# Edge ranks from (window, segment) partitions and a segment pick, in a one-core graph network kernel

## The chip, the cores and the metric

The kernel runs on one core of a Trainium2 chip. The metric is device time in microseconds, the median of three runs. Times of single instructions come from one profiled execution of the same program.

## The reference

One layer of a graph network with 3125 nodes of 64 features, 53125 edges (25000 in both directions and a self loop at each node) and hidden width 128. Every edge has a source `src`, a destination `dst` and a weight.

```
h   = silu(concat(x[src], x[dst], edge_weight) @ eW1 + eb1)   # 53125 x 128
m   = silu(h @ eW2 + eb2)                                     # 53125 x 128
agg = segment_sum(m, src, 3125)
y   = silu(concat(x, agg) @ nW1 + nb1) @ nW2 + nb2
out = layernorm(x + y)
```

The random `src` is not sorted, so the sum over edges needs the edges brought into an order by source on the chip.

## The kernel before

**Layout.** The edges lie on 125 partitions (EP) and 425 columns (ECOL). The columns are cut into 9 chunks, `LOAD = [50, 30, 38, 44, 48, 54, 54, 54, 53]`. A node's number is 25 x `lo` + window, 25 windows (WIN) in all. A counting sort on the chip brings the edges of a window together in tiles of 128 slots (SLOT). There are 440 tiles in 110 groups of four (GT). For every tile GpSimd gathers 128 rows of the table `q_table` (x times the destination half of eW1) by an indirect DMA; TensorE adds the source half by one-hot products with `p_table`, runs the two edge layers and sums each tile's edges into its window (`segment`), which VectorE adds into `agg`.

**Parts of the sort.** `part(name, k, i)` issues a step of the sort of chunk k, on VectorE and on TensorE. On VectorE, before:

- MATCH (line 1048) compares every edge's window `win_b` with the 25 windows: `in_win`, 25 x columns elements on each of the 125 partitions.
- SCAN (1061) is a running sum over `in_win`, two instructions: `count`.
- TOTAL (1065 to 1070) takes the end of each window's run: `total`, `rank`.
- TensorE's OFFSET multiplies `total` by `before` (earlier partitions) and by `ones` (all of them).
- OFFSET (1074 to 1093) makes `base`: the first place of each window in each partition, with the tile in multiples of ENC = 8192.
- SUM adds `base` to `count` (1105), multiplies by `in_win` (1109, 1110) and reduces over the 25 windows (1111), in two halves of the columns: `slot`.
- SLOTS (1116 to 1126) splits this into tile, row and column; DEST and WINDOW place the chunk's tiles in the order of windows.
- SORT makes one-hots of column and row for batches of six columns (`col_hot` 1209, `row_hot` 1210, `load_hot` 1215) in a ring of three; TensorE's `sort(k, i)` multiplies them. CLOSE ends the chunk's product, READ takes the gather indices `q_index` (1247) and the weights out.

**Order.** The tables VECTOR and TENSOR, written by `plan()`, say at which of the 110 steps a part stands on its engine. At step m TensorE issues `second_layer(m-2)`, `first_layer(m)`, `turn(m+2)`, `segment(m-4)` and then its parts; VectorE issues `one_hots(m+3)`, `add_segments(m-5)` and its parts. `first_layer(m)` reads the four gathered tiles of group m. GpSimd's buffer holds four groups, so the gathers of group g wait for the first layer of step g-4; a new chunk waits for `index_ready`, group 2 for chunk 1's offsets and group 3 for chunk 1's WINDOW as well.

**Start.** ScalarE loads its table, clears `agg` and copies results. TensorE transposes x (line 795), takes OFFSET of chunk 0 after the first of the P/Q products (`pq`, `less`), runs these for 13 pairs of windows, and from slot 10 on puts chunk 0's sort batches between them. ScalarE copies each P/Q result out (534, 536), and among these copies writes the columns of `load` (489) that VectorE's first sort batch needs. GpSimd derives the node numbers of chunks 1 to 8 (713 to 722) once VectorE's first one-hots are done (`hots_ready`).

Of the kernel before, what the change touches and what calls it, by code (L numbers as in the profile page):

```python
# [31 lines left out]
EVEN = [n + n % 2 for n in LOAD]  # L32
# [17 lines left out]
CMAX, NMAX, BATCH = max(COLS), max(EVEN), 6  # L50
V = 4
# [3 lines left out]
WSPLIT = [(0, HALF), (HALF, WIN)]  # L55
# [9 lines left out]
assert sum(LOAD) == ECOL and TILES % GT == 0 and all(n % 2 == 0 for n in LOAD[:-1]) and V * CMAX <= 512  # L65
# [10 lines left out]
def batches(k):  # L76
# [27 lines left out]
def plan():  # L104

    at(TENSOR, 0, (CARRY, 1, 0))
    sorts(1, [0, 0, 0, 1, 1], [0, 0, 0, 1, 1])
    at(TENSOR, 1, (CLOSE, 1, 0))
    at(VECTOR, 2, (READ, 1, 0), (MATCH, 2, 0), (SCAN, 2, 0))
    at(VECTOR, 3, (SCAN, 2, 1), (TOTAL, 2, 0), (ENCODE, 2, 0))  # L110
    at(TENSOR, 3, (OFFSET, 2, 0))
    at(VECTOR, 4, (OFFSET, 2, 0), (SUM, 2, 0))
    at(TENSOR, 4, (DEST, 2, 0))
    at(VECTOR, 5, (SUM, 2, 1), (DEST, 2, 0), (SLOTS, 2, 0))
# [3 lines left out]
    sorts(2, [5, 6, 6, 7, 7, 8, 8], [6, 6, 7, 7, 8, 8, 8])  # L118
    at(TENSOR, 8, (CLOSE, 2, 0))
    at(VECTOR, 9, (READ, 2, 0), (MATCH, 3, 0), (SCAN, 3, 0), (SCAN, 3, 1), (TOTAL, 3, 0))  # L120
    at(TENSOR, 9, (OFFSET, 3, 0))
    at(VECTOR, 10, (OFFSET, 3, 0), (SUM, 3, 0))
    at(TENSOR, 10, (DEST, 3, 0))
    at(VECTOR, 11, (DEST, 3, 0), (SUM, 3, 1))
    at(TENSOR, 11, (WINDOW, 3, 0))
    at(VECTOR, 12, (WINDOW, 3, 0), (SLOTS, 3, 0))
    at(TENSOR, 12, (CARRY, 3, 0))
    sorts(3, [12, 12, 13, 13, 14, 15, 15, 16], [13, 13, 14, 14, 15, 16, 16, 16])
    at(TENSOR, 16, (CLOSE, 3, 0))

    at(VECTOR, 17, (READ, 3, 0), (MATCH, 4, 0))
    at(VECTOR, 18, (SCAN, 4, 0), (SCAN, 4, 1), (TOTAL, 4, 0))
    at(TENSOR, 18, (OFFSET, 4, 0))
    at(VECTOR, 19, (OFFSET, 4, 0), (SUM, 4, 0))
    at(TENSOR, 19, (DEST, 4, 0))
    at(VECTOR, 20, (DEST, 4, 0), (SUM, 4, 1))
    at(TENSOR, 20, (WINDOW, 4, 0))
    at(VECTOR, 21, (SLOTS, 4, 0), (WINDOW, 4, 0))
    at(TENSOR, 21, (CARRY, 4, 0))
    sorts(4, [21, 22, 22, 23, 24, 24, 25, 26], [22, 23, 23, 24, 25, 25, 26, 27])  # L140
    at(TENSOR, 27, (CLOSE, 4, 0))
# [78 lines left out]
def build(nc, x, src, dst, edge_weight, eW1, eb1, eW2, eb2, nW1, nb1, nW2, nb2, out):  # L220
    with ExitStack() as ctx:
# [6 lines left out]
        def sem(name):  # L228
# [10 lines left out]
        iota_w = sb("iota_w", [EP, WIN, 2], BF16)  # L239
# [6 lines left out]
        before = sb("before", [128, 128])  # L246
        ones = sb("ones", [128, 128])
# [28 lines left out]
        win_b = sb("win_b", [EP, ECOL + 1], BF16)  # L276
# [68 lines left out]
        window_ps = [t[0:1, 128:256] for t in flat_ps]  # L345

# [19 lines left out]
        iota_w_c = const_ps[0:EP, 128:128 + WIN].bitcast(BF16).rearrange("p (b e) -> p b e", e=2)  # L366
        base_c = const_ps[0:EP, 160:160 + WIN]
# [3 lines left out]
        def load_c(c):  # L371
# [7 lines left out]
                 "totals_ready offsets_ready dest_ready dests_ready upto_ready window_ready window_read rest_ready restT_ready "  # L379
# [6 lines left out]
         totals_ready, offsets_ready, dest_ready, dests_ready, upto_ready, window_ready, window_read, rest_ready, restT_ready,  # L386
# [8 lines left out]
        FILLS = 6  # L395
# [70 lines left out]
        def _(act):  # L466
# [10 lines left out]

            act.wait_ge(fills_ready, 1)
# [60 lines left out]
            for i in range(PQ_SLOTS):  # L539
# [93 lines left out]
            load_coded(1)  # L633
            for m in range(GROUPS):
# [55 lines left out]
        def _(pool):  # L690
# [4 lines left out]
            fills = [(ones[:], 1.0), (run_prev[:], 0.0), (carried[:], 0.0), (win_b[:, ECOL:ECOL + 1], -1.0),  # L695
# [53 lines left out]
        def _(pe):  # L749
# [71 lines left out]
            for i in range(PQ_SLOTS):  # L821
# [164 lines left out]
        def _(dve):  # L986
# [11 lines left out]
            def then(ins):  # L998
                done(mark(ins))
# [437 lines left out]
```

## Time and profile before

| what | us |
|---|---|
| median of 3 runs (lowest, highest) | 629.42 (627.53, 630.96) |
| the profiled execution | 630.7 |
| its span | 628.9 |
| TensorE busy | 533.6 (85%) |
| VectorE busy | 462.9 (74%) |
| GpSimd busy | 430.5 (68%) |
| ScalarE busy | 355.5 (57%) |

The span runs from the first to the last instruction of the profiled execution; the run's own time is 1.8 us longer. Busy shares are means over the whole span. GpSimd's busy time holds neither the issue of its gathers nor its waits. What a stage is bound by is read from windows of time and from what ended each wait.

### The profile page before, as it was taken

What the parts mean: (1) busy time and instruction counts of PE and PEld (TensorE: products, weight loads), DVE (VectorE), ACT (ScalarE), POOL (GpSimd) and SP (SyncE); (2) the same over time, 40 slices, a digit from 0 to 9 for tenths busy, and PEclk for the clock granted to TensorE, in tenths of its full rate; (3) what the DMA queues carried; (4) which work ended last, traced back from release to release, by engine and by line L of the source; (5) the groups of instructions that cost most, each with busy time, mean ns of one, the idle gap of its engine ahead of it and who ended that gap; (6) DMA issues with size and microseconds to landing.
All of it is one profiled execution on the core that took longest, in us unless ns stands there. A gap on an engine that the chain in (4) does not pass through costs nothing.

```text
span 628.9 us, 15166 instructions
## 1 busy us (share of the span) xinstructions
PE 533.6 (85%) x4653; PEld 449.0 (71%) x4653; DVE 462.9 (74%) x1364; ACT 355.5 (57%) x812; POOL 430.5 (68%) x465
## 2 busy tenths in 40 slices
PE   3953979779889979999998899889997888879695
PEld 2432768758768868887787788778776777769584
DVE  5998999988999898999788868797642533223356
ACT  4852555535645656665555555565556666556464
POOL 2327677566777777777777777777777777777750
PEclk9985889879989999999999999999999999999998
DMA  5121111111211112212121112111221212111111
GB/s 121 58 63 53 48 51 53 39 46 48 56 52 52 53 51 56 55 49 55 53 56 52 55 51 58 53 54 51 56 53 55 56 52 55 52 55 56 52 39 51
DMA packets 17215, 34.17 MB, mean 54 GB/s; under 512 B 8133, under 2 KB 9352, under 8 KB 17142
## 3 DMA queue, kind: packets, MB, share of 16 engines
q0 software_dynamic: 14080, 28.86, 16.8%
q1 hardware_dynamic: 2594, 3.40, 2.1%
q10 hardware_dynamic: 468, 0.96, 0.6%
q8 instruction: 43, 0.70, 0.5%
q14 instruction: 30, 0.25, 0.1%
HBM read 30.73 MB, written 2.40 MB: 53 GB/s over the span
## 4 chain that ended last, share of the span: by engine, by line
POOL 33%; DVE 27%; PE 18%; issue 16%; DMA 4%; DVEq 2%; ACTq 0%; SPq 0%
POOL q_rows L738 33%; PE layer_ps L751 7%; PE sort_ps L751 5%; PE seg_ps L751 4%; DVE load_hot L1215 3%; DVE agg L1286 3%; DMA q_rows<-q_table,q_index 3%; DVE hot L1271 2%; DVE count L1061 2%; DVE place L1105 2%; DVE col_hot L1209 1%; DVE row_hot L1210 1%; DMA x_sb<-in_x_dram 1%; DVEq L1278 1%; DVE slot L1111 1%
## 5 line engine op out<-in xcount | busy, mean ns | idle before, releaser
L738 POOL DMA_INDIRECT q_rows<-q_table,q_index x440 | 420.8, 956 | 155.0 <-issue 128.5
L585 ACT ACTIVATE e<-layer_ps 128x512 f32<-128x512 f32 x110 | 65.7, 597 | 212.5 <-PE seg_ps L751 207.4
L1286 DVE TENSOR_TENSOR agg<-agg,seg_ps 128x125 f32 x416 | 93.1, 280 | 95.2 <-PE seg_ps L751 92.0
L751 PE MATMUL layer_ps<-hotT,p_table 128*128 128x128 bf16 x1320 | 160.0, 225 | 0.1
L751 PE MATMUL layer_ps<-ident_f,q_rows 128*128 128x128 f32 x440 | 127.1, 289 | 34.7 <-DMA q_rows<-q_table,q_index 34.2
L751 PE MATMUL seg_ps<-hot,e 128*128 128x125 f32 x880 | 124.6, 285 | 19.4 <-DVE agg L1286 19.3
L751 PEld LDWEIGHTS layer_ps<-hotT,p_table 128*128 x1320 | 122.8, 99 | 23.6 <-issue 2.3
L751 PEld LDWEIGHTS seg_ps<-hot,e 128*128 128x128 f32 x880 | 109.0, 195 | 22.5 <-issue 20.3
L751 PE MATMUL layer_ps<-w_sb,h 128*128 128x128 f32 x880 | 120.0, 280 | 0.0
L751 PEld LDWEIGHTS layer_ps<-w_sb,h 128*128 128x128 f32 x880 | 111.6, 194 | 4.7 <-issue 0.2
L751 PEld LDWEIGHTS layer_ps<-ident_f,q_rows 128*128 128x128 f32 x440 | 63.3, 144 | 45.6 <-DMA q_rows<-q_table,q_index 43.8
L1215 DVE TENSOR_TENSOR load_hot<-col_hot,const_ps 125x2448 bf16<-125x2448 bf16 (+9 forms) x73 | 93.7, 1283 | 0.0
L751 PE MATMUL sort_ps<-load_hot,row_hot 125*128 125x408 bf16 (+5 forms) x425 | 82.7, 336 | 9.5 <-DVE load_hot L1215 9.5
L579 ACT ACTIVATE h<-layer_ps,eb_sb 128x512 f32<-128x512 f32 x110 | 76.0, 691 | 16.3 <-PE layer_ps L751 16.2
L565 ACT ACTIVATE hot<-hot 128x500 f32<-128x500 bf16 x110 | 69.0, 628 | 0.0
L624 ACT ACTIVATE layer_ps<-b_sb 128x512 f32<-128x512 f32 x110 | 67.0, 609 | 0.1
L573 ACT ACTIVATE hotT<-turn_ps 128x512 bf16<-128x512 bf16 x110 | 64.9, 590 | 3.7 <-PE turn_ps L843 3.7
L751 PEld LDWEIGHTS sort_ps<-load_hot,row_hot 125*128 125x128 bf16 x425 | 41.6, 101 | 34.7 <-issue 9.3
L1271 DVE TENSOR_TENSOR hot<-const_ps,lo 128x512 bf16<-128x512 bf16 x110 | 45.9, 418 | 24.7 <-ACT hot L565 24.0
L843 PE MATMUL turn_ps<-ident_b,hot 128*128 128x128 bf16 x440 | 43.6, 223 | 0.9 <-ACT hot L560 0.8
L1210 DVE TENSOR_TENSOR row_hot<-const_ps,row 125x768 bf16<-125x768 bf16 (+2 forms) x73 | 39.0, 535 | 0.0
L1209 DVE TENSOR_TENSOR col_hot<-const_ps,col 125x612 bf16<-125x612 bf16 (+9 forms) x73 | 31.9, 437 | 2.6 <-PE sort_ps L751 2.0
(193 smaller groups left out, 432.1 us busy)
## 6 DMA issues: line engine op xcount, KB each, us to landing
q_rows<-q_table,q_index POOLq DMA_INDIRECT x440
q_table<-q_in_sb SPq DMA_DIRECT2D x1, 784.0 KB
x_sb<-in_x_dram ACTq DMA_DIRECT2D x1, 700.0 KB
q_table<-q_in_sb SPq DMA_DIRECT2D x1, 616.0 KB
out_dram<-x_sb SPq DMA_DIRECT2D x2, 224.0 KB
out_dram<-x_sb SPq DMA_DIRECT2D x1, 252.0 KB
w_in<-in_edge_weight_dram SPq DMA_DIRECT2D x1, 185.9 KB
dst_i<-in_dst_dram SPq DMA_DIRECT2D x1, 185.9 KB
```

Source lines behind the costliest of these rows:

```text
L565: A.activation(hot32[:, g % 4], hot[:, g % HOT_RING, :, 0:LO], ACT.Copy).then_inc(hot32_ready, 1)
L573: A.activation(hotT[:, g % TURNED, :], hotT_ps, ACT.Copy).then_inc(hotT_ready, 1)
L579: A.activation(h1[:, m % 2, :], pre_of(m)[:], ACT.Silu, bias=eb1_sb[:, 0:1]).then_inc(h1_ready, 1)
L585: A.activation(e2[:, m % 2, :], e_of(m)[:], ACT.Silu).then_inc(e2_ready, 1)
L624: A.activation(e_of(m)[:].rearrange("p (j f) -> p j f", j=GT), b2_sb[:].unsqueeze(1).to_broadcast([128, GT, HID]), ACT.Copy).then_inc(bias ...
L738: P.indirect_dma_start(q_rows[:, g % RING, j, :], None, q_table, bass.IndirectOffsetOnAxis(ap=q_index[:, GT * g + j:GT * g + j + 1], axis= ...
L751: return nc.tensor.matmul(o, lhsT, rhs, start=start, stop=stop, **kw)
L843: last = nc.tensor.transpose(hotT_ps[:, j * 128:(j + 1) * 128], hot[:, g % HOT_RING, j, :], ident_b[:])
L1210: D.tensor_tensor(pairs(row_hot[:, q, 0:m, :]), iota(SLOT), each(row2[:, a:a + m, :], SLOT), ALU.is_equal).then_inc(hots_ready, 1)
L1215: D.tensor_tensor(load_hot[:, q, 0:m, :, 0:c].rearrange("p m v (a b) -> p m v a b", b=2), pairs(col_hot[:, q, 0:m, 0:c]).unsqueeze(2).to_b ...
L1271: D.tensor_tensor(pairs(hot[:, g % HOT_RING]), iota1_c.rearrange("p (a b) -> p a b", b=2).unsqueeze(1).to_broadcast([128, GT, 64, 2]), lo2 ...
L1286: D.tensor_tensor(o, o, seg_ps[:, j * LO:(j + 1) * LO], ALU.add).then_inc(agg_added, 1)
```

## The change

The 125 partitions stand for 25 windows times SEG = 5 segments of the columns when ranks are counted, instead of for 125 rows of edges.

- A chunk's windows `win_b` are transposed by TensorE (`turn_windows`), chunk 0 as its first instruction, chunks 1 to 8 ahead of chunk 0's third last sort batch. `spread_windows` multiplies them by `column_sel`, a table of ones that ScalarE writes at the start, LOAD/5 products of 125 x 125: after that every partition (segment, window) sees all edges of its segment. ScalarE copies the result from PSUM into `spread` (chunk 0 is read from PSUM by VectorE).
- MATCH compares with one number for each partition (`win_col`); `in_win` has 25 x columns elements as before. SCAN is one instruction with f32 output, TOTAL one operation. OFFSET has two operations more (`own`, `base_col`); its product uses `upto_sel` in place of `before`.
- SUM becomes two `scalar_tensor_tensor` operations, (count + base_col) x in_win. TensorE's `pick(k)` reduces over windows and brings the places back to edge order: LOAD/5 f32 products of 125 x 125 by 125 x 5 (`seg_sel`). SLOTS reads them from PSUM; it waits for `slots_ready` and, from chunk 1 on, for `dests_ready`.
- `LOAD` is `[50, 30, 45, 50, 50, 50, 50, 50, 50]`, and `plan()` follows: chunk 3's READ is at step 18 (17 before), chunk 4's at 29 (28 before).
- GpSimd's derivation of later node numbers waits no more for `hots_ready`, only for the landed data.

```diff
-LOAD = [50, 30, 38, 44, 48, 54, 54, 54, 53]
+SEG = 5
+LOAD = [50, 30, 45, 50, 50, 50, 50, 50, 50]
...
             pool.wait_ge(src_rest_in, 32)
-            pool.wait_ge(hots_ready, 1)
...
+            act.wait_ge(ident_ready, 2)
+            A.activation(column_sel[:], ident_b[0:NMAX, 0:NMAX].unsqueeze(2).to_broadcast([NMAX, NMAX, WIN]), ACT.Copy) \
+                .then_inc(column_sel_ready, 1)
             act.wait_ge(fills_ready, 1)
             clear(agg[0])
...
+            def turn_windows(chunks):
+                for k in chunks:
+                    last = nc.tensor.transpose(win_t_ps(k), win_b[:, COL0[k]:COL0[k] + NMAX], ident_b[0:EP, 0:EP])
+                last.then_inc(win_t_ready, 1)
+            def spread_windows(k, i):
+                pe.wait_ge(win_turned, 1 + (k > 0))
+                if k >= 2:
+                    pe.wait_ge(w_parted, k - 1)
+                    pe.wait_ge(spread_read, fill_of(k, i) - 1)
+                sel = column_sel[:].rearrange("q c b -> q (c b)")
+                for t0, n, bank in spread_columns(k, i):
+                    for t in range(n):
+                        last = mm(bank[:, t, :], sel[0:LOAD[k], (t0 + t) * EP:(t0 + t + 1) * EP], win_t[0:LOAD[k], k, :], True, True)
+                last.then_inc(spread_made, 1)
+            def pick(k):
+                n = segments(k)
+                for t in range(n):
+                    if t in (0, n // 2):
+                        pe.wait_ge(place_ready, 2 * k + 1 + (t > 0))
+                    last = mm(slot_ps[k % 2][:, t * SEG:(t + 1) * SEG], count[:, t * EP:(t + 1) * EP], seg_sel[:], True, True)
+                last.then_inc(slots_ready, 1)
...
                 elif name == SUM:
-                    halves = [(0, m // 2), (m // 2, m)]
...
+                    half = segments(k) // 2 * EP
+                    for a, b in ((0, half), (half, wide)):
+                        D.scalar_tensor_tensor(count[:, a:b], count[:, a:b], base_col[:, 0:1], in_win[:, a:b],
+                                               ALU.add, ALU.mult).then_inc(place_ready, 1)
```

At the start of TensorE's program, before: x is transposed, then `sort_ps<-total` is OFFSET of chunk 0, and `layer_ps<-w_sb,xT` are the P/Q products.

```order
L795 MATMUL layer_ps<-ident_f,x_sb 128x125 x12
L795 MATMUL seg_ps<-ident_f,x_sb 64x125
L751 MATMUL layer_ps<-w_sb,xT 125x512
L751 MATMUL sort_ps<-total,before 125x25
L751 MATMUL sort_ps<-total,ones 125x25
L751 MATMUL layer_ps<-w_sb,xT 125x512
L751 MATMUL layer_ps<-p_table,minus_b 125x256
```

In the changed kernel the same place reads so; `win_t,column_sel` is the spread and `seg_sel,count` the pick.

```order
L829 MATMUL turn_ps<-ident_b,win_b 50x125
L812 MATMUL sort_ps<-win_t,column_sel 125x125 x8
L812 MATMUL turn_ps<-win_t,column_sel 125x125 x2
L896 MATMUL layer_ps<-ident_f,x_sb 128x125 x8
L812 MATMUL sort_ps<-total,upto_sel 125x25
L812 MATMUL sort_ps<-total,ones 125x25
L896 MATMUL layer_ps<-ident_f,x_sb 128x125 x4
L896 MATMUL seg_ps<-ident_f,x_sb 64x125
L812 MATMUL layer_ps<-w_sb,xT 125x512
L812 MATMUL sort_ps<-seg_sel,count 125x5 x10
L812 MATMUL layer_ps<-w_sb,xT 125x512
```

OFFSET has moved ahead of the last five transposes of x, and the pick stands between the first and the second P/Q product.

At step 0 TensorE had, ahead of its first layer (`layer_ps<-ident_f,q_rows`), the turn of chunk 0's rest and OFFSET of chunk 1:

```order
L846 MATMUL turn_ps<-ident_b,rest 100x128
L751 MATMUL sort_ps<-total,before 125x25
L751 MATMUL sort_ps<-total,ones 125x25
L855 TENSOR_LOAD p_at
L751 MATMUL layer_ps<-ident_f,q_rows 128x128
```

In the changed kernel there stand at the same place the pick, DEST (`tiles_upto`, `dest_row`) and WINDOW (`ge`) of chunk 1 and the first spread of chunk 2 as well:

```order
L951 MATMUL turn_ps<-ident_b,rest 100x128
L812 MATMUL sort_ps<-total,upto_sel 125x25
L812 MATMUL sort_ps<-total,ones 125x25
L812 MATMUL sort_ps<-seg_sel,count 125x5 x6
L812 MATMUL sort_ps<-ones,tiles_upto 25x1
L812 MATMUL sort_ps<-ones,dest_row 100x1
L812 MATMUL sort_ps<-ge,ones 1x55
L812 MATMUL sort_ps<-win_t,column_sel 125x125 x4
L960 TENSOR_LOAD p_at
L812 MATMUL layer_ps<-ident_f,q_rows 128x128
```

DEST and WINDOW of chunk 1 have moved from behind step 0's work to ahead of its first layer.

On VectorE the sum of chunk 0 was, between the offset arithmetic and the first operation of SLOTS (`tile`):

```order
L1081 SCALAR_TENSOR_TENSOR base<-tiles_upto,base 125x25
L1105 TENSOR_TENSOR place<-count,base 125x625 x2
L1109 TENSOR_TENSOR place<-place,in_win 125x325
L1110 TENSOR_TENSOR place<-place,in_win 125x300
L1111 TENSOR_REDUCE slot<-place 125x25
L1109 TENSOR_TENSOR place<-place,in_win 125x325
L1110 TENSOR_TENSOR place<-place,in_win 125x300
L1111 TENSOR_REDUCE slot<-place 125x25
L1116 TENSOR_SCALAR tile<-slot 125x50
```

In the changed kernel there stands instead:

```order
L1197 SCALAR_TENSOR_TENSOR base<-tiles_upto,base 125x25
L1198 TENSOR_TENSOR own<-base,win_sel 125x25
L1199 TENSOR_REDUCE base_col<-own 125x1
L1223 SCALAR_TENSOR_TENSOR count<-count,base_col,in_win 125x625 x2
L1232 TENSOR_SCALAR tile<-sort_ps 125x50
```

Eight operations have become four, and `tile` reads TensorE's result.

## Rows read from the trace of the kernel before

**Rows 1.** GpSimd's timeline: start us, duration us, instruction, idle before and its releaser.

```profile
41.48 1.17 POOL L738 DMA_INDIRECT q_rows<-q_table,q_index  x1 [9.80 <-DVE q_index L1247]
...
119.17 0.95 POOL L738 DMA_INDIRECT q_rows<-q_table,q_index  x1 [3.55 <-PE seg_ps L751]
...
199.66 0.94 POOL L738 DMA_INDIRECT q_rows<-q_table,q_index  x1 [0.30 <-issue]
...
606.53 0.94 POOL L738 DMA_INDIRECT q_rows<-q_table,q_index  x1 [0.30 <-issue]
```

**Rows 2.** Waits of GpSimd, whole span: us in total, times, longest.

```profile
POOL q_rows L738 <- PE seg_ps L751: 14.7, 16, 3.5
```

**Rows 3.** Busy time by stretch: us, each engine's busy us, PEclk, DMA share, GB/s.

```profile
41.50:150.00 108.50, 81.23 (x689) 67.72 (x690) 100.04 (x312) 51.15 (x120) 74.85 (x78) 0.83 0.18 48
...
290.00:470.00 180.00, 166.44 (x1476) 139.82 (x1475) 141.65 (x395) 101.52 (x227) 136.13 (x144) 1.00 0.20 54
...
16.58:28.08 11.50, 11.50 (x40) 4.96 (x39) 11.09 (x26) 11.15 (x41) 1.89 (x3) 1.00 0.24 79
```

The engines stand in the order PE, PEld, DVE, ACT, POOL.

**Rows 4.** TensorE's timeline, columns as in rows 1.

```profile
9.95 2.76 PE L795 MATMUL layer_ps<-ident_f,x_sb 125*128 125x125 f32 x12 [9.95 <-DMA x_sb<-in_x_dram]
...
14.42 0.46 PE L751 MATMUL sort_ps<-total,before 125*125 125x25 f32 x2
15.13 1.51 PE L751 MATMUL layer_ps<-w_sb,xT 128*125 128x512 f32 x2
16.58 1.02 PE L751 MATMUL layer_ps<-w_sb,xT 128*125 128x512 f32 x2
...
28.08 0.94 PE L751 MATMUL sort_ps<-load_hot,row_hot 125*128 125x296 bf16 x6
...
32.67 0.94 PE L751 MATMUL sort_ps<-load_hot,row_hot 125*128 125x296 bf16 x6
...
113.39 0.40 PE L751 MATMUL sort_ps<-total,before 125*125 125x25 f32 x2 [3.22 <-DVE total L1069]
...
619.52 1.04 PE L751 MATMUL turn_ps<-n_sb,load_hot 128*125 128x64 f32 x8
```

**Rows 5.** ScalarE's timeline in the first 22 us, columns as in rows 1.

```profile
6.54 2.81 ACT L476 ACTIVATE agg<-ones 128x3125 f32<-128x3125 f32 x1
...
21.14 0.66 ACT L489 ACTIVATE load<-enc_i 125x100 bf16<-125x100 bf16 x3
```

**Rows 6.** VectorE's groups by line and form, 109 to 131 us: busy us, mean ns.

```profile
L1111 DVE TENSOR_REDUCE slot<-place 125x22 f32<-125x550 f32 x2 | 2.7, 1330 | 0.1
L1105 DVE TENSOR_TENSOR place<-count,const_ps 125x550 f32<-125x550 bf16 x2 | 1.4, 725 | 0.0
L1109 DVE TENSOR_TENSOR place<-place,in_win 125x286 f32<-125x286 f32 x2 | 0.9, 444 | 0.0
```

**Rows 7.** VectorE's timeline up to the first index, columns as in rows 1.

```profile
6.38 2.81 DVE L1061 TENSOR_TENSOR_SCAN count<-sort_ps,in_win 125x650 bf16<-125x650 f32 x2
...
15.34 0.18 DVE L1074 TENSOR_TENSOR summed<-carried,sort_ps 125x25 f32<-125x25 f32 x1 [3.48 <-PE sort_ps L751]
...
22.52 0.19 DVE L1116 TENSOR_SCALAR tile<-slot 125x50 f32<-125x50 f32 x1
...
24.62 0.37 DVE L1199 COPY const_ps<-load 125x200 f32<-125x200 f32 x1
...
37.28 0.38 DVE L1209 TENSOR_TENSOR col_hot<-const_ps,col 125x444 bf16<-125x444 bf16 x1
...
40.40 0.21 DVE L1247 TENSOR_SCALAR q_index<-sort_ps 128x49 int32<-128x49 int32 x1 [0.58 <-PE sort_ps L751]
```

**Rows 8.** Page, costliest groups: count, busy us, mean ns of one, idle before.

```profile
L1215 DVE TENSOR_TENSOR load_hot<-col_hot,const_ps 125x2448 bf16<-125x2448 bf16 (+9 forms) x73 | 93.7, 1283 | 0.0
...
L1210 DVE TENSOR_TENSOR row_hot<-const_ps,row 125x768 bf16<-125x768 bf16 (+2 forms) x73 | 39.0, 535 | 0.0
L1209 DVE TENSOR_TENSOR col_hot<-const_ps,col 125x612 bf16<-125x612 bf16 (+9 forms) x73 | 31.9, 437 | 2.6 <-PE sort_ps L751 2.0
```

More of the change, by code:

```diff
@@ L64 @@
 TAG = 1 << 29
-assert sum(LOAD) == ECOL and TILES % GT == 0 and all(n % 2 == 0 for n in LOAD[:-1]) and V * CMAX <= 512
+assert sum(LOAD) == ECOL and TILES % GT == 0 and all(n % SEG == 0 for n in LOAD) and SEG * WIN == EP and V * CMAX <= 512
 assert all(EP * COL0[k] // SLOT + FULL[k] <= TABLE for k in range(CHUNKS)) and EP * max(LOAD) + SLOT <= 8000
@@ L77, in batches @@
     return [(a, min(BATCH, LOAD[k] - a)) for a in range(0, LOAD[k], BATCH)]
-MATCH, SCAN, TOTAL, OFFSET, SUM, SLOTS, DEST, WINDOW, SORT, READ, CARRY, CLOSE, ENCODE, NODE_X, RESIDUAL, CARRIED = (
-    "match", "scan", "total", "offset", "sum", "slots", "dest", "window", "sort", "read", "carry", "close", "encode",
-    "node_x", "residual", "carried")
+SPREAD, MATCH, SCAN, TOTAL, OFFSET, SUM, PICK, SLOTS, DEST, WINDOW, SORT, READ, CARRY, CLOSE, ENCODE, NODE_X, RESIDUAL, CARRIED = (
+    "spread", "match", "scan", "total", "offset", "sum", "pick", "slots", "dest", "window", "sort", "read", "carry", "close",
+    "encode", "node_x", "residual", "carried")
 VECTOR, TENSOR = {}, {}
@@ L944, in _ @@
                     part(OFFSET, 1, 0)
+                    pick(1)
+                    part(DEST, 1, 0)
+                    part(WINDOW, 1, 0)
+                    spread_windows(2, 0)
                 first = first_layer(m)
@@ L1081, in part @@
                         then(D.scalar_tensor_tensor(base[:], tiles_upto[:], float(ENC), base[:], ALU.mult, ALU.add))
+                        then(D.tensor_tensor(own[:], base[:], win_sel[:], ALU.mult))
+                        then(D.tensor_reduce(base_col[:], own[:], AX.X, ALU.add))
                         return
@@ L1353, in _ @@
             encode(*CODED[0])
-            for name, i in ((OFFSET, 0), (SUM, 0), (SUM, 1), (SLOTS, 0)):
+            for name, i in ((OFFSET, 0), (SUM, 0), (SLOTS, 0)):
                 part(name, 0, i)
@@ L1365, in _ @@
             dve.wait_ge(rest_coded, 2)
-            for name, i in ((ENCODE, 0), (MATCH, 0), (SCAN, 0), (SCAN, 1), (TOTAL, 0), (OFFSET, 0), (SUM, 0), (DEST, 0), (SUM, 1),
-                            (SLOTS, 0), (WINDOW, 0)):
+            for name, i in ((MATCH, 0), (SCAN, 0), (TOTAL, 0), (ENCODE, 0), (OFFSET, 0), (SUM, 0), (SLOTS, 0), (DEST, 0),
+                            (WINDOW, 0)):
                 part(name, 1, i)
```

258 lines of the change are left out of this document (160 added, 98 removed).

## The prediction

> **What bounds the kernel now.** Read first the busy time by stretch, then GpSimd's waits and its row of gathers, then each engine's timeline up to the first gather.
>
> GpSimd issues 440 gathers, the first at 41.48 us, the last at 606.53 [rows 1]. A gather takes 0.94 us and the next follows after 0.30 of issue: 1.25 us each. So the span of 628.9 is 41.48 of prologue, 439 x 1.25 = 548.75 of gathers at full pace, 16.3 of excess over that pace, 0.94 for the last gather and 21.4 of tail. A change gains only by bringing the first gather forward, by taking from the 16.3, or in the tail, which this change leaves alone.
>
> Where the excess arises is read by index: gather 56 (group 14) starts at 119.17, that is 7.7 us behind 41.48 + 56 x 1.25; gather 116 (group 29) at 199.66, 13.2 behind [rows 1]. The last 3.1 come in 400 us, from somewhat longer gathers. TensorE ended 16 waits of GpSimd, 14.7 us with 4.8 of ordinary issue in them [rows 2]; with one more on a transpose, some 11.3 us are true waiting. The cause stands behind TensorE: VectorE is busy 100.04 of the 108.5 us after the first gather [rows 3], and the 3.55 us before gather 56 follow a TensorE queue that stood 3.22 us on VectorE's totals of chunk 3 [rows 1, 4]. After 290 us VectorE has slack (141.65 of 180) and TensorE, though 166.44 busy, ends no gather wait of weight.
>
> **The prologue: what is added.** VectorE can no longer match straight after its node numbers. TensorE turns and spreads them first, and its spread needs `column_sel` from ScalarE. ScalarE's first activation started at 6.54 and wrote 3125 columns in 2.81 [rows 5], 0.9 ns a column; the 1250 of `column_sel` end at about 7.85. Ten spread products at 0.14 us (six of 296 columns take 0.94 [rows 4]; bounds 1.1 to 2.1 in all) end at 9.25. The match reads 1250 f32 elements from PSUM: 0.73 us for 550 [rows 6] makes 1.5. The scan keeps its 1250 elements, 2.81 [rows 7], and ends at 13.75; its output is f32 now, which I price at nothing because the scan's own pace of 2.2 ns an element is far above any write seen here. Total at 13.95. Before, totals were ready by 9.9 and TensorE came for them only at 14.42 [rows 4], so this delay alone costs nothing there.
>
> The order on TensorE does cost. After totals: OFFSET 0.9, five x transposes 1.1 (twelve took 2.76), the first P/Q product 1.7: 17.7. VectorE's offset arithmetic took 1.28 from 15.34 to the sum; with two new short operations it ends at 16.6, and two `scalar_tensor_tensor` of 625 elements at 0.8 end at 18.2. Then come ten `pick` products ahead of the second P/Q product. The trace has no product with five moving columns. An f32 product is two passes; eight passes of 64 columns took 1.04, 0.13 each; two of 25 columns 0.40 to 0.46, no less [rows 4]. Early passes run slower (1.51 against 1.02 for the same pair [rows 4]). So 20 passes cost 2.6 to 3.9 us; I take 3.2, the middle, since the pace changes just there. End: 20.9.
>
> The Trainium skill, TensorE: Matmul & The Clock Gate, section LDWEIGHTS (loading the stationary operand), says that a weight load takes time by the stationary operand's columns, P/1.2 ns, whatever moves. That is 104 ns for 125 columns, 2.1 us for 20 passes as an estimate; the sum below would be 626.7 by it. The trace agrees that few columns don't make a pass cheap, but its passes are longer.
>
> The second P/Q product thus starts at 20.9 instead of 15.13; the product now runs at the full pace, 0.5 back: 5.3 late. TensorE was busy for all of the 11.50 us up to chunk 0's first sort [rows 3], so nothing absorbs the shift: that sort goes from 28.08 to 33.4, the third from 32.67 to 38.0 (done 38.8). VectorE makes the one-hots in a ring of three, so its sixth batch waits for the third sort. Before, VectorE ran free: first copy at 24.62, then 1.75 a batch, the eighth at 37.28 [rows 7]. The sixth thus began at 33.78, and now at 38.8: 5.0 late. ScalarE's load columns (21.14 [rows 5]) move by 5.3 as well, to 27.1 when written, later than VectorE's slots, which start 1.4 earlier than 22.52 [rows 7]; the ring is later still and decides. The first index, 40.40 [rows 7], moves by 5.1 with the turns and the second spread hidden in TensorE's gaps between VectorE-paced batches. **Prologue +5.1**, bounds +2.5 (pick at 2.6, spread at 1.1, VectorE at once behind) to +7.3 (pick at 3.9, spread at 2.1, and 0.7 for turns and spread that are not hidden). GpSimd's node work beside the scan is in these bounds: it has only to be done by the seventh sort batch, and it touches the chain only if it slows the 2.81 us scan.
>
> **The loop: what is removed.** For chunk 3, the sum was two adds of 0.725, four products of some 0.44 and two reductions of 1.33 [rows 6]: 5.9 us. Now two operations of 0.8. Totals take one operation instead of five (0.46 less), the base two more (0.4): 4.3 less on VectorE. But chunks grow: a batch of six columns costs 1.28 + 0.54 + 0.44 = 2.26 [rows 8], 0.38 a column. Chunk 2 gets seven more: 3.6 saved, 3.0 given back. Chunk 3 gets six more: 4.3 saved at steps 9 to 12, 2.6 back at steps 13 to 16. Chunk 1 saves 3.1 and gives back 1.5 on the wait for `pick`. Chunk 4, two columns more, saves 4.0. So VectorE is ahead by some 2.3 us at step 9, 6 at step 13, 4 at step 17 and 8 at step 28.
>
> New on the other side: DEST, WINDOW and `pick` of chunk 1 now stand ahead of step 0's first layer on TensorE, and chunk 1's offsets on VectorE come before them. Group 3 waits for them. I put this wait at 3.0 us, from VectorE's match, scan, sum and slots of chunk 1 against the 15 us of the first three groups (bounds 1 to 6).
>
> The excess by group 14 is then 7.7 - 2.3 = 5.4, since the 3.0 of group 3 lie within it; by group 18 the old value of about 11.5 less 6 gives the same 5.5; with 1 us for what chunk 3's extra batch costs around step 17 it is 6.5 by group 29 instead of 13.2. **Loop -6.7**, bounds -2 (the wait of group 3 at its upper end, and chunk waits that stay) to -11.3 (all waits gone).
>
> TensorE pays 4.5 us more a chunk for spread and pick (about 30 passes). Steps with no sorting have that room after 290 us: 13.6 us in 180 are idle, and one chunk falls in about 65 us; I cost it at nothing, and at up to 2 us if gathers do wait.
>
> **Sum.** +5.1 - 6.7 = -1.6: 627.3 of span, 629.1 for the profiled run of 630.7. That run lay 1.3 above the median of 629.42, from which the forecast is 627.8.
>
> **The rivals.**
> B, faster: the spread and pick are at their low ends and all waits of GpSimd go. For it: every such wait lies before 200 us, where VectorE is full [rows 2, 3]. Against: TensorE's order at step 0. +2.5 - 11.3 = -8.8: 620.6.
> C, slower: TensorE's strict order turns the new waits into the bound. Prologue +7.3, and step 0 behind chunk 1's `pick` and WINDOW keeps the waits, so that the loop returns 2: 634.7. It decides from the point where the first index is later by more than the loop gives back. For it: ring and queue pass the shift of the P/Q products on entirely; against: VectorE is measurably relieved of reductions that stood on the path.
> D, the change doesn't do what it says: the larger chunks' one-hots and the waits for `pick` use up the saved VectorE time, the loop returns nothing, +5.1: 634.5. Against: the saving of chunk 3 falls before its larger cost.
> That TensorE becomes the bound after 290 us is priced above: with the 2 us it gives 629.8, inside the forecast's own range.
>
> **How the numbers follow.** Forecast 0.52, B 0.27, C 0.14, D 0.07. The likeliest case's own range is 625 to 631 (pick and spread by their bounds, group 3's wait between 1 and 5). The whole range, 619.5 to 634.5, takes in B and stops short of about half of C. About 0.5%, 3.1 us, is what a measurement of this kernel can tell from no change: faster is below 626.3, slower above 632.6. Of the forecast's 0.52 some 0.12 lie below, 0.38 within, 0.02 above; B gives 0.26 faster and 0.01 same; C and D 0.19 slower and 0.02 same. Faster 0.38, same 0.41, slower 0.21.
>
> **What would show it.** The first gather at about 46.6 us (44 to 48.8); if it stays near 41.5, the chain from `pick` over P/Q to the sort ring was wrong. The ten `pick` products at 3.2 us, and the second P/Q product at about 21. Totals before 14.5. GpSimd's waits on TensorE at about 5 us instead of 11.3, the first of them at group 3. Gather 116 some 6.5 behind full pace. VectorE some 5 us per chunk less busy with sums. The forecast falls if the first layer of step 0 stands more than 6 us behind chunk 1, or if TensorE ends gather waits after 200 us.

## The result: 1.5% slower, and the profile after

The changed kernel takes 638.45 us, median of four runs (636.3 to 640.91), against 629.07 of the kernel before in the same comparison: a ratio of 1.0149, interval 1.0102 to 1.0196. The forecast was 627.8, its range ended at 634.5. In a second comparison it took 640.19 against 630.16, a ratio of 1.0150 (1.0121 to 1.0179). The profiled execution took 639.05, its span is 637.1.

GpSimd's timeline of the changed kernel answers to [rows 1]: start, duration, and in brackets the idle time before and what ended it.

```profile
49.27 1.16 POOL L799 DMA_INDIRECT q_rows<-q_table,q_index  x1 [31.82 <-DVE q_index L1363]
...
68.95 0.94 POOL L799 DMA_INDIRECT q_rows<-q_table,q_index  x1 [4.75 <-PE turn_ps L948]
...
120.92 0.94 POOL L799 DMA_INDIRECT q_rows<-q_table,q_index  x1 [1.88 <-PE seg_ps L812]
...
128.52 0.94 POOL L799 DMA_INDIRECT q_rows<-q_table,q_index  x1 [2.91 <-PE seg_ps L812]
...
136.06 0.94 POOL L799 DMA_INDIRECT q_rows<-q_table,q_index  x1 [2.85 <-PE seg_ps L812]
...
614.47 0.95 POOL L799 DMA_INDIRECT q_rows<-q_table,q_index  x1 [0.30 <-issue]
```

The first gather is 7.79 us later than before. From there to the last one the excess over full pace (439 x 1.25 us) is 614.47 - 49.27 - 548.75 = 16.45 us; before it was 16.3. The tail is 0.3 longer. So nearly all of the span's 8.2 us are the prologue, and the loop has given nothing back: the excess arises at other places, at group 3 (4.75 us of idle time) and at groups 13 to 15, and is the same in sum. A profile is one execution: in that of the second comparison (640.59 us) the first gather came at 51.90 and the excess was 16.03.

Busy time in the 108.5 us after the first gather, the stretch of the first line in [rows 3] (PE, PEld, DVE, ACT, POOL, then PEclk, DMA share and GB/s):

```profile
49.30:157.80 108.50, 91.89 (x765) 78.00 (x766) 96.25 (x289) 54.03 (x127) 73.84 (x78) 0.84 0.18 48
```

VectorE is only 3.8 us less busy there than before (96.25 against 100.04), and idle for 3.8 more. What it waits for, in us, times, longest:

```profile
DVE tile L1232 <- PE sort_ps L812: 5.9, 3, 2.9
DVE q_index L1363 <- PE sort_ps L812: 1.2, 2, 1.0
```

The first line is SLOTS waiting for the pick of chunks 1, 2 and 3 (2.91, 1.46 and 1.56 us): a wait that did not exist.

Where VectorE's lead is lost is seen from the first operation of chunk 2's SLOTS (`tile`) to its index and on to the totals of chunk 3; first the kernel before, then the changed one:

```profile
87.13 0.36 DVE L1116 TENSOR_SCALAR tile<-slot 125x38 f32<-125x38 f32 x1
...
107.25 0.22 DVE L1247 TENSOR_SCALAR q_index<-sort_ps 128x61 int32 x1
...
113.15 0.19 DVE L1069 TENSOR_TENSOR total<-run_end,run_prev 125x25 f32<-125x25 f32 x1
```

```profile
92.10 0.21 DVE L1232 TENSOR_SCALAR tile<-sort_ps 125x45 f32<-125x45 f32 x1 [1.46 <-PE sort_ps L812]
...
116.66 0.23 DVE L1363 TENSOR_SCALAR q_index<-sort_ps 128x69 int32 x1 [0.19 <-PE sort_ps L812]
...
122.45 0.24 DVE L1186 TENSOR_SCALAR total<-win_sel,count 125x25 f32<-125x25 f32 x1
```

Counted from the first gather, VectorE begins these SLOTS 2.8 us earlier than before (42.83 against 45.65), but has the index 1.6 us later (67.39 against 65.77) and the totals 1.5 later (73.18 against 71.67). Busy time between SLOTS and index, columns as above, before and changed:

```profile
87.13:107.25 20.12, 17.95 (x153) 15.12 (x152) 19.61 (x55) 9.89 (x22) 14.60 (x16) 0.92 0.19 50
```

```profile
92.10:116.66 24.56, 24.56 (x203) 20.21 (x203) 23.60 (x61) 12.75 (x28) 18.66 (x20) 0.90 0.21 55
```

VectorE is 4.0 us longer busy there for seven more columns, and TensorE, which stood idle for 2.2 us, is busy all the time.

The prologue on TensorE, which answers to [rows 4]:

```profile
14.66 0.59 PE L812 MATMUL sort_ps<-total,upto_sel 125*125 125x25 f32 x2 [3.09 <-DVE total L1186]
...
16.57 1.92 PE L812 MATMUL layer_ps<-w_sb,xT 128*125 128x512 f32 x2
19.21 2.35 PE L812 MATMUL sort_ps<-seg_sel,count 125*125 125x5 f32 x20 [0.72 <-DVE count L1223]
21.42 1.52 PE L812 MATMUL layer_ps<-w_sb,xT 128*125 128x512 f32 x2
...
22.95 1.91 PE L812 MATMUL layer_ps<-w_sb,xT 128*125 128x512 f32 x2
...
35.40 0.94 PE L812 MATMUL sort_ps<-load_hot,row_hot 125*128 125x296 bf16 x6
...
39.99 0.94 PE L812 MATMUL sort_ps<-load_hot,row_hot 125*128 125x296 bf16 x6
```

The second P/Q product starts at 21.42 (15.13 before, 20.9 forecast). The third one still takes 1.91 us, where the kernel before ran it in 1.02 [rows 4]. The granted clock is 0.50 here, the level of 1.2 GHz, against 1.00, that of 2.4 GHz, in 16.58 to 28.08 before [rows 3]:

```profile
22.00:25.00 3.00, 3.00 (x7) 1.22 (x6) 1.50 (x9) 1.04 (x4) 0.00 (x0) 0.50 0.00 0
```

The way from the second P/Q product to the first sort is therefore 13.98 us long, not 12.95.

VectorE in the same place, beside GpSimd's node numbers:

```profile
11.29 2.76 DVE L1182 TENSOR_TENSOR_SCAN count<-sort_ps,in_win 125x1250 f32<-125x1250 f32 x1
14.09 0.43 DVE L1186 TENSOR_SCALAR total<-win_sel,count 125x25 f32<-125x25 f32 x1
...
16.03 0.37 DVE L1192 TENSOR_SCALAR rounded<-summed 125x25 f32<-125x25 f32 x1
...
16.65 0.87 DVE L1194 TENSOR_TENSOR_SCAN tiles_upto<-ones,tiles 125x25 f32<-125x25 f32 x1
...
18.29 1.65 DVE L1223 SCALAR_TENSOR_TENSOR count<-count,base_col,in_win 125x625 f32<-125x625 f32 x2
```

GpSimd's timeline shows the six operations on node numbers in just this stretch; the first, the third and the last two:

```profile
11.76 0.50 POOL L774 CAST node_f<-src_i 125x375 f32<-125x375 int32 x1 [7.47 <-DMA src_i<-in_src_dram]
...
12.96 1.53 POOL L778 TENSOR_SCALAR lo_f<-lo_t 125x375 f32<-125x375 f32 x1
...
15.84 0.53 POOL L781 TENSOR_SCALAR enc_t<-lo_f 125x375 int32<-125x375 f32 x1
16.45 1.00 POOL L783 TENSOR_TENSOR win_b<-lo_t,node_f 125x375 bf16<-125x375 f32 x1
```

### The profile page after: what moved, and what is told of

Read it like the earlier page. It is cut to its first block, busy times and chain, and to the rows that moved or that the text cites. A ratio compares the mean times of both kernels' runs of the same rounds, so it can differ in the third digit from the quotient of the medians.

```text
span 637.1 us, 15701 instructions
## 1 busy us (share of the span) xinstructions
PE 568.0 (89%) x4917; PEld 481.9 (76%) x4917; DVE 427.6 (67%) x1298; ACT 367.7 (58%) x837; POOL 429.1 (67%) x463
## 3 DMA queue, kind: packets, MB, share of 16 engines
q0 software_dynamic: 14080, 28.86, 17.2%
## 4 chain that ended last, share of the span: by engine, by line
POOL 37%; PE 32%; issue 15%; DVE 12%; DMA 2%; ACT 1%; DVEq 1%; ACTq 0%; SPq 0%
POOL q_rows L799 37%; PE layer_ps L812 14%; PE sort_ps L812 10%; PE seg_ps L812 6%; DMA q_rows<-q_table,q_index 2%; DVE load_hot L1331 2%; DVE count L1182 2%; PE turn_ps L948 1%; DVE agg L1402 1%; DVE col_hot L1325 1%; DVE row_hot L1326 1%; DVE hot L1387 1%; DVE count L1223 0%; DVEq L1394 0%; DVE stat L1448 0%
## 5 line engine op out<-in xcount | busy, mean ns | idle before, releaser
L812 PE MATMUL layer_ps<-hotT,p_table 128*128 128x128 bf16 x1320 | 162.1, 229 | 0.2
L812 PE MATMUL layer_ps<-ident_f,q_rows 128*128 128x128 f32 x440 | 129.7, 295 | 25.4 <-DMA q_rows<-q_table,q_index 25.0
L812 PEld LDWEIGHTS layer_ps<-hotT,p_table 128*128 x1320 | 125.2, 101 | 22.5 <-issue 1.9
L812 PE MATMUL layer_ps<-w_sb,h 128*128 128x128 f32 x880 | 124.3, 286 | 0.2 <-ACT layer_ps L683 0.2
L1331 DVE TENSOR_TENSOR load_hot<-col_hot,const_ps 125x2352 bf16<-125x2352 bf16 (+5 forms) x76 | 93.6, 1232 | 0.0
L812 PEld LDWEIGHTS layer_ps<-ident_f,q_rows 128*128 128x128 f32 x440 | 65.0, 148 | 35.8 <-DMA q_rows<-q_table,q_index 34.3
L638 ACT ACTIVATE h<-layer_ps,eb_sb 128x512 f32<-128x512 f32 x110 | 76.0, 691 | 16.5 <-PE layer_ps L812 16.5
L812 PE MATMUL sort_ps<-load_hot,row_hot 125*128 125x392 bf16 (+3 forms) x425 | 78.4, 322 | 3.2 <-DVE load_hot L1331 3.2
L1326 DVE TENSOR_TENSOR row_hot<-const_ps,row 125x768 bf16<-125x768 bf16 (+1 forms) x76 | 39.5, 520 | 0.0
L1325 DVE TENSOR_TENSOR col_hot<-const_ps,col 125x588 bf16<-125x588 bf16 (+5 forms) x76 | 32.3, 424 | 3.2 <-PE sort_ps L812 2.6
```

What stands on the lines that cost most here:

```text
L638: A.activation(h1[:, m % 2, :], pre_of(m)[:], ACT.Silu, bias=eb1_sb[:, 0:1]).then_inc(h1_ready, 1)
L812: return nc.tensor.matmul(o, lhsT, rhs, start=start, stop=stop, **kw)
L1326: D.tensor_tensor(pairs(row_hot[:, q, 0:m, :]), iota(SLOT), each(row2[:, a:a + m, :], SLOT), ALU.is_equal).then_inc(hots_ready, 1)
L1331: D.tensor_tensor(load_hot[:, q, 0:m, :, 0:c].rearrange("p m v (a b) -> p m v a b", b=2), pairs(col_hot[:, q, 0:m, 0:c]).unsqueeze(2).to_b ...
```

## The experiments

The theory, A, had two halves. The prologue is late by TensorE's order: the queue stands still for the totals and the sum while the P/Q chain waits behind. The loop gains nothing because larger chunks and new waits take back what VectorE saved. The rivals, B, are named in each expectation.

### Pick later in the prologue

```diff
-                if n == 2:
-                    pe.wait_ge(consts_ready, 1)
-                    pe.wait_ge(fills_ready, FILLS)
-                    part(OFFSET, 0, 0)
...
                 if i == 0:
+                    pe.wait_ge(consts_ready, 1)
+                    pe.wait_ge(fills_ready, FILLS)
+                    part(OFFSET, 0, 0)
+                if i == 3:
                     pick(0)
```

> Of the changed kernel only TensorE's order in the prologue differs: all transposes of x and the first P/Q product stand ahead of OFFSET of chunk 0, and the ten pick products stand after the fourth P/Q slot instead of the first. Same work. Theory A (TensorE's strict order makes the late first index: it stood idle 3.09 us for the totals and 0.72 us for the sum, and the P/Q chain waited behind): the second P/Q product goes from 21.4 back to about 15.5, chunk 0's first sort from 35.40 to about 31, the first gather from 49.27 to about 44.7, the span by 4 to 5 us, time near 634. Rival B (the added products and the slow pace cost as much wherever they stand): first gather stays within 1.5 us of 49.27, time 637 or more.

Measured: 634.26, ratio 1.0068 to the kernel before (1.0045 to 1.0090). Its timeline of TensorE and the first gather:

```profile
15.48 2.05 PE L812 MATMUL layer_ps<-w_sb,xT 128*125 128x512 f32 x2
...
20.36 2.24 PE L812 MATMUL sort_ps<-seg_sel,count 125*125 125x5 f32 x20
```

```profile
45.48 1.17 POOL L799 DMA_INDIRECT q_rows<-q_table,q_index  x1 [28.05 <-DVE q_index L1363]
```

The second P/Q product is back at 15.48 and the first gather comes 3.8 us earlier with the same work; the time's interval lies below that of the changed kernel. A holds for the order. Of the 7.8 us of the prologue about 4 stay, and not all of that is the added products' time: with GpSimd's wait restored as well (the three edits together) 2.3 stay.

### The first layer of step 0 ahead of chunk 1's pick

```diff
                 if m == 0:
                     part(OFFSET, 1, 0)
-                    pick(1)
-                    part(DEST, 1, 0)
-                    part(WINDOW, 1, 0)
-                    spread_windows(2, 0)
                 first = first_layer(m)
...
+                if m == 0:
+                    pick(1)
+                    part(DEST, 1, 0)
+                    part(WINDOW, 1, 0)
+                    spread_windows(2, 0)
```

> Of the changed kernel only step 0 on TensorE differs: the first layer and the turn of step 0 stand behind OFFSET of chunk 1 and ahead of its pick, DEST, WINDOW and the first spread of chunk 2. GpSimd's 4.75 us wait at group 3 should fall to about 2.3. Theory A (VectorE's chain over chunks 1 to 3, with larger chunks, sets the excess by group 15 whatever stood before): the excess over full pace at group 15 stays at about 11.8 and the time at 638. Rival B (the wait at group 3 adds to the later ones): excess at group 15 falls by 2.4 and the time to about 636.

Measured: 639.58, ratio 1.0135 (1.0114 to 1.0157), not to be told from the changed kernel. The excess at group 3 fell from 4.7 to 1.9 us, at group 14 it was 10.0 (9.2 in the changed kernel) and at group 15 12.6 (11.8). The 2.8 us gained at group 3 are lost again by group 15. The wait at group 3 is real, but it is not added to the others: A.

### GpSimd waits again for the first one-hots

```diff
             pool.wait_ge(src_rest_in, 32)
+            pool.wait_ge(hots_ready, 1)
```

> Of the changed kernel only GpSimd's derivation of the later node numbers waits again for VectorE's first one-hots, as before the change. Theory A (GpSimd's operations at 11.8 to 17.4 us slow VectorE's totals and offsets of chunk 0 beside them, 0.43 for the totals and 0.87 for a scan of 25 that took 0.21 before): the sum of chunk 0 starts some 1.1 us earlier than 18.29, and the first gather 0.7 to 1.1 us earlier. Rival B (the slower operations have another cause, or don't reach the chain): first gather within 0.3 us of 49.27, time unchanged.

Measured: 635.16, ratio 1.0111 (1.0071 to 1.0152). VectorE's timeline with GpSimd silent beside it:

```profile
13.99 0.24 DVE L1186 TENSOR_SCALAR total<-win_sel,count 125x25 f32<-125x25 f32 x1
...
16.16 0.21 DVE L1194 TENSOR_TENSOR_SCAN tiles_upto<-ones,tiles 125x25 f32<-125x25 f32 x1
...
17.14 1.65 DVE L1223 SCALAR_TENSOR_TENSOR count<-count,base_col,in_win 125x625 f32<-125x625 f32 x2
```

TensorE's pick and the P/Q product behind it:

```profile
18.07 2.50 PE L812 MATMUL sort_ps<-seg_sel,count 125*125 125x5 f32 x20
20.43 1.10 PE L812 MATMUL layer_ps<-w_sb,xT 128*125 128x512 f32 x2
```

The sum starts 1.15 us earlier, as A says; the first gather of this profile, at 46.84, is 2.4 earlier, more than A's 0.7 to 1.1. TensorE no longer waited for the sum ahead of the pick, and the pairs of P/Q passes behind the pick took 1.0 to 1.1 us at once. On VectorE, then, the derivation beside its short operations was a loss. Its size in the time is not settled: the interval overlaps that of the changed kernel, the five times reach from 633.96 to 639.87, and the profiled execution is the fastest of them.

### The three edits together

> The three edits together: pick late in the prologue, first layer of step 0 ahead of chunk 1's pick and WINDOW, GpSimd's wait for the one-hots restored. Theory A (prologue by order, loop by VectorE's chain): only the prologue's gain is seen, first gather at 44 to 45, time 633 to 634.5, still slower than the kernel before by 0.6% or more. Rival B (every edit adds its own gain): 630 or less, at or below the kernel before.

Measured: 633.26, ratio 1.0041 (1.0023 to 1.0059). First gather at 43.79, 2.3 us behind the kernel before. The excess at group 15 was 11.1, at the end 17.2: the prologue's gain is seen, the loop's is not, as A says.

### The chunk sizes alone, in the kernel before

```diff
-LOAD = [50, 30, 38, 44, 48, 54, 54, 54, 53]
+LOAD = [50, 30, 46, 50, 50, 50, 50, 50, 49]
...
-    at(VECTOR, 17, (READ, 3, 0), (MATCH, 4, 0))
+    at(VECTOR, 18, (READ, 3, 0), (MATCH, 4, 0))
```

> The kernel before with the chunk sizes of the change alone: 50, 30, 46, 50, 50, 50, 50, 50, 49 columns, and the steps of chunks 2 to 4 placed as the change places them (READ of chunk 3 at step 18, of chunk 4 at 29). Theory A (VectorE's work per chunk, larger by 8 and 6 columns at chunks 2 and 3, sets the excess of GpSimd's gathers): excess at group 19 rises from 11.6 to 15 or 16, time about 634 to 635. Rival B (sizes don't matter, since the total of columns is the same): excess 11.6 and 630.

Two of the sizes are one column off those of the change (46 and 49 for 45 and 50).

Measured: 636.49, ratio 1.0098 (1.0067 to 1.0129). The first gather came at 40.80, the last at 612.04: an excess of 22.5 us instead of 16.3. GpSimd's waits (us, times, longest), against 14.7 in [rows 2]:

```profile
POOL q_rows L738 <- PE seg_ps L751: 24.5, 20, 4.7
```

So the new sizes cost the old sort 6 us, more than A expected (19.0 of excess by group 19 instead of 15 or 16). VectorE's totals of chunk 3 stood 77.5 us after the first gather, before it was 71.7.

### The old chunk sizes in the changed kernel

```diff
-LOAD = [50, 30, 45, 50, 50, 50, 50, 50, 50]
+LOAD = [50, 30, 38, 44, 48, 54, 54, 53, 54]
...
-            return LOAD[k] // SEG
+            return -(-LOAD[k] // SEG)
...
-                    mark(D.tensor_tensor(win_mul[:], win_sel[:], iota_f[0:EP, 0:WIN], ALU.mult))
+                    mark(D.tensor_tensor(win_mul[:], win_sel[:], iota_f[0:EP, 1:1 + WIN], ALU.mult))
```

Windows count from 1 here, so that the columns that fill up a segment (0 after the spread) match none.

> The changed kernel with the old chunk sizes (50, 30, 38, 44, 48, 54, 54, 53, 54; segments are filled up with columns that match no window) and the old steps. Prologue as in the changed kernel, first gather near 49. Theory A (the larger chunks have eaten what VectorE saved): excess at group 19 falls from 11.8 to about 7, at the end from 16.5 to about 11, time to 633 or 634. Rival B (the round trips to TensorE for OFFSET and pick, not the columns, hold the chain): excess at group 19 stays above 11, time 637 or more.

Measured: 635.95, ratio 1.0084 (1.0056 to 1.0112). The excess was 9.4 at group 19 and 12.4 at the end instead of 16.45: A in its direction, with half of its size at group 19 and some three quarters at the end; the time lies between A's 633 or 634 and B's 637. The five profiles with the loop of the changed kernel (its own two, and those in which only the prologue was edited) have an excess of 14.4 to 16.5, so that the old sizes give 2 to 4 us. The first gather of this profile came at 51.98; the last experiment shows TensorE's two paces, with which it moves from one execution to the next. VectorE in the 108.5 us after it, and what it waited for:

```profile
52.00:160.50 108.50, 90.48 (x785) 77.82 (x786) 91.08 (x287) 55.44 (x129) 75.59 (x80) 0.86 0.19 49
```

```profile
DVE tile L1234 <- PE sort_ps L814: 5.6, 3, 2.9
```

At equal sizes the change does save VectorE 9.0 us in this stretch (100.04 to 91.08). The larger chunks take back 5.2 of them (96.25), and 5.6 to 5.9 are spent waiting for the pick. Of the 9.0 us some 4 reach the gathers (excess 16.3 before, 12.4 here). VectorE begins chunk 2's SLOTS 42.60 us after the first gather, 3.05 earlier than the kernel before, and has the index at 65.67, only 0.1 earlier. In between it is busy for 20.39 us and TensorE for the whole time:

```profile
94.58:117.65 23.07, 23.07 (x196) 19.47 (x196) 20.39 (x59) 12.20 (x28) 17.58 (x19) 0.89 0.20 54
```

So with the columns of before, too, the lead is lost, beside a TensorE that has no idle time left. That TensorE is the reason is read from this trace alone; no run takes its added products away.

### All edits and the old sizes

> All edits together: pick late in the prologue, first layer of step 0 ahead of chunk 1's pick, GpSimd's wait restored, and the old chunk sizes. Theory A: first gather at 43.8, excess at group 19 about 6 and about 11 at the end; 628, some 0.4% faster than the kernel before. Rival B: excess at group 19 still 11, 633 as without the old sizes.

Measured: 627.61, ratio 0.9966 (0.9952 to 0.9981): faster than both kernels, by 0.34% against the kernel before. First and last gather:

```profile
43.58 1.16 POOL L801 DMA_INDIRECT q_rows<-q_table,q_index  x1 [12.94 <-DVE q_index L1366]
...
603.15 0.94 POOL L801 DMA_INDIRECT q_rows<-q_table,q_index  x1 [0.30 <-issue]
```

The prologue is 2.1 us longer than before, the excess 10.8 instead of 16.3. The sum of both is -3.4 in this profile, -2.6 in the medians (627.61 against 630.17): this is what the change brought with all four edits. The sizes are worth 6.4 us of excess here (17.2 with the new ones, 10.8 with the old) against 4.0 without the other edits, but in the ratios 0.75% against 0.65%: that they are worth more here is not shown.

### The changed kernel again, and with TensorE kept busy

The first of the two is the changed kernel as it is. The second adds products that nobody reads:

```diff
                 if n == 2:
+                    for _ in range(18):
+                        mm(seg_ps[:, 0:128], ident_b[:], ident_b[:], True, True)
                     pe.wait_ge(consts_ready, 1)
...
                 if i == 0:
+                    for _ in range(4):
+                        mm(turn_ps[:, 256:384], ident_b[:], ident_b[:], True, True)
                     pick(0)
```

> The changed kernel itself, once more, beside the next one. Time about 638, first gather between 49 and 53 us.

> The changed kernel with more work on TensorE in its two idle places of the prologue: 18 products of 128 bf16 columns ahead of OFFSET of chunk 0 (it stood idle 3.09 us there) and 4 ahead of chunk 0's pick (0.72 us idle); nobody reads them. Theory A (the idle places bring TensorE to its slow pace, and the P/Q chain behind them runs at it until about 25 us or later): pick stays near 2.3 us, the P/Q products of 512 columns take about 1.0 a pair instead of 1.5 to 1.9, and the first gather comes at 46.5 to 48 us although more work is done, time 1.5 to 4 us lower than the changed kernel beside it. Rival B (the pace has nothing to do with the idle places): first gather no earlier, or later by what the added products overrun, time equal or higher.

Measured: 640.19 (ratio 1.0150) and 638.19 (1.0133, 1.0109 to 1.0158). TensorE in the first:

```profile
14.53 0.59 PE L812 MATMUL sort_ps<-total,upto_sel 125*125 125x25 f32 x2 [2.28 <-DVE total L1186]
...
16.44 1.92 PE L812 MATMUL layer_ps<-w_sb,xT 128*125 128x512 f32 x2
19.37 4.36 PE L812 MATMUL sort_ps<-seg_sel,count 125*125 125x5 f32 x20 [1.01 <-DVE count L1223]
23.59 2.05 PE L812 MATMUL layer_ps<-w_sb,xT 128*125 128x512 f32 x2
```

and in the second:

```profile
15.52 1.02 PE L812 MATMUL layer_ps<-w_sb,xT 128*125 128x512 f32 x2
...
18.66 2.58 PE L812 MATMUL sort_ps<-seg_sel,count 125*125 125x5 f32 x20 [1.90 <-DVE count L1227]
21.11 2.05 PE L812 MATMUL layer_ps<-w_sb,xT 128*125 128x512 f32 x2
```

The same pick takes 2.35 us in one execution of the changed kernel and 4.36 in the other. With the added products the first P/Q product runs in 1.02 instead of 1.92 us, the pick in 2.58, and the first gather comes at 48.97 instead of 51.90. TensorE then comes to the pick earlier and stands 1.90 us for the sum, and the products behind it are slow again (2.05). So the idle places ahead do matter for the pace: the first pair is fast without one and the pair behind 1.90 us of idle time is slow. They are not the whole of it, since with the pick late the second pair took 2.05 us behind only 0.33 of idle time. A's first gather at 46.5 to 48 was missed: 48.97 is hardly earlier than the 49.27 of the first execution. As a remedy it gains too little to be told apart by the times, whose intervals overlap.

## Why the prediction was wrong

**The frame held.** First gather, excess and tail were the right three terms, and the first two moved as separate things: 7.8 and 0.15 us, forecast 5.1 and -6.7. Of the 9.8 us by which the span was missed, 2.7 are the prologue's and 6.9 the loop's.

**Prologue, +5.1 forecast, +7.8 measured.** The chain was the right one: pick ahead of the second P/Q product, then the sorts, then the ring. Three sizes were off. VectorE's offsets ran beside GpSimd, and its sum started at 18.29 instead of 16.6; the forecast had dismissed that cover by saying that it matters only if the long scan is slowed. The scan was not (2.76), the short operations behind it were. The pace of TensorE was assumed to be full behind the pick (0.5 gained); it was slow there, and the way to the first sort became 1.0 longer instead. And the spread of chunk 1 was said to lie in a gap; it stands between the last two sort batches, and the last sort, hence the index, came 0.5 later for it (third sort +7.3, index +7.8). The pick took 2.35 us for the forecast's 3.2 in this profile, 0.118 a pass, but 4.36 in three others with the same prologue, more than the forecast's upper bound of 3.9: the forecast took the middle of two paces, and its slow one, 0.195 a pass, was not slow enough (0.218). By the Trainium skill, TensorE: Matmul & The Clock Gate, section LDWEIGHTS (loading the stationary operand), 104 ns a pass are the estimate; the better pace of 0.118 lies between it and the row of 0.13 of the forecast's lower bound.

**Loop, -6.7 forecast, +0.15 measured.** Here steps failed, not sizes alone. The first of them: the forecast took VectorE's lead off the excess of the gathers us for us. With the old sizes 9.0 us saved on VectorE became some 4 at the gathers (one profile each), so this step was wrong even without the larger chunks. Two terms were missing in it. The waits for the pick were charged to chunk 1 only, at 1.5 us; VectorE stood 5.9 us for three chunks. The forecast had named `pick` as a product that TensorE must run and not as a round trip that VectorE's next operation waits for in every chunk. And TensorE's spread and pick were put at nothing, with room that was read after 290 us; in the 108.5 us after the first gather TensorE is 10.7 us longer busy than before (91.89 against 81.23), and among chunk 2's sort batches it has no idle time at all.

The VectorE terms themselves were nearer: 11.0 us saved and 5.6 given back by the end of chunk 3 were forecast, 9.0 and 5.2 were measured in the stretch. (Three small terms hold 0.2 to 0.3 us more than the rows they name: the end of `column_sel`, 7.85 where 6.54 + 1250 x 0.9 ns give 7.67; the end of the scan, 13.75 where 9.25 + 1.5 + 2.81 give 13.56; and the larger chunks, 3.0 and 2.6 where seven and six columns at 0.38 give 2.7 and 2.3. None of them changes the outcome.) But a lead of 2.3 us was forecast for step 9, where chunk 2's index is read, and VectorE was 1.6 us behind there. It had been 2.8 ahead at chunk 2's SLOTS, with two of the waits for the pick behind it, and lost the lead among the one-hots of seven more columns, 4.0 us of VectorE's time for 3.0 forecast, beside a full TensorE. So the totals of chunk 3, for which TensorE stands at step 9, came 73.2 us after the first gather (122.45 - 49.27), 1.5 later than the 71.7 before, and the waits of groups 13 to 15 stayed, 7.6 us of idle time in the three rows above. How the loss splits between the waits for the pick, the larger chunks and TensorE is shown for the chunks alone (2 to 4 us); the rest is read from the traces. The wait at group 3 was forecast at 3.0 and was 4.75; that it would lie within the later ones was right, as the run with the first layer ahead shows.

**The rivals.** Between C and D: the prologue of C (its 7.3 is short by 0.5), and the loop that returns nothing of D, whose reasons, larger chunks and waits for the pick, are among those measured. They had 0.21 together, and their sum, +7.3 with a loop of 0, which is 636.7, was never formed. C joined the bad ends of both halves, but a loop that returns nothing lay outside the loop's bounds; D had it, with the middle of the prologue. TensorE as a new bound after 290 us did not come (it was full earlier, among the sort batches): it is busy 172.06 of the 180 us from 300 on, 5.6 more than before in 290 to 470 [rows 3], and from group 29 on the excess grows by 2.9 us, before by 3.1.

**What stays open.** It is open how the 8.2 us of the changed kernel split between order, GpSimd's neighbourhood and pace: the edits overlap (together -5.5 at the first gather, singly -3.8 and -2.4), and the first gather of four profiles with the same prologue lay between 49.27 and 52.70. Nor is it shown how much of the loop's loss the waits for the pick and TensorE's added products make, each by itself. Whether smaller chunks than the old ones would serve the shorter VectorE chain was not tried.

## What to carry to other kernels

Work moved from a bound engine to another one becomes a round trip: price the wait of the first engine for the answer in every repetition, not the helper's busy time. A relief that is used at once for larger pieces, here chunks of 45 and 50 columns instead of 38 and 44, has to be tested with the old sizes first: with them, and the other three edits, a loss of 9.4 us became a gain of 2.6. And in a strict queue, put the products that wait for another engine behind those that can already run.

## What the runs showed of the hardware

Short VectorE operations took longer beside GpSimd's operations on 375 columns: 0.87 us instead of 0.21 for a scan of 25, 0.43 instead of 0.24 for the totals. Each ended within 0.1 us of the end of a GpSimd operation: the totals at 14.52 (GpSimd's at 14.49), the rounding at 16.40 (16.37), the scan at 17.52 (17.45). A scan of 1250 elements with one input in PSUM was not slower (2.76 both ways). The Trainium skill, GPSIMD Engine Reference, section 8. Key points, says that GpSimd shares its SBUF interfaces with VectorE and contends with instructions that have two SBUF inputs or run in a two-port mode; this trace agrees for the scans: that of 25 has two SBUF inputs, the long one has one. The totals and the rounding read one tensor each and were slowed too; no row shows in which mode they ran.

TensorE's passes in the prologue ran at two paces: 1.92 and 1.02 us for the same pair of 512 columns, 4.36 and 2.35 for the same 20 passes of 5 columns. In the changed kernel the slow pace came behind 2.3 to 3.1 us of idle time, and filling that time with products that nobody reads brought the first pair to 1.02; with the pick late a slow pair stood behind 0.33 us. The granted clock shows the two in one place, 0.50 from 22 to 25 us with a pair at 1.91, but not everywhere. The busy time of the second execution of the changed kernel by stretch (PE, PEld, DVE, ACT, POOL, PEclk, DMA share, GB/s):

```profile
20.00:25.00 5.00, 5.00 (x20) 4.29 (x21) 1.19 (x7) 0.00 (x0) 0.00 (x0) 1.00 0.00 0
```

It shows 1.00, the level of 2.4 GHz, for a stretch in which the pick and the second P/Q product ran at half the pace of others; so the pace was read from the passes. Why the two differ is open.

A pass of 5 moving columns costs 0.118 us at the better pace and 0.218 at the slower one; one of 64 costs 0.13 [rows 4].
